# Splitting the context part from the expert part, and halving the first chain, in a one-core attention and expert kernel

## The chip, the core and the metric

The kernel runs on one core of one Trainium2 chip. The metric is the device time of one execution in microseconds. Every matrix and every intermediate is 32-bit float.

## The reference

```
B, T, D = 4, 512, 256                     # batches, tokens, width
# 1. conditioned bottleneck with residual, gain and offset per batch from cond (4, 128)
w_down = down_project * (cond @ down_gamma) + cond @ down_beta       # 256 x 64 per batch
w_up   = up_project * (cond @ up_gamma) + cond @ up_beta             # 64 x 256 per batch
h = relu(x @ w_down) @ w_up + x
# 2. attention over "paths": 8 heads, depth 5, causal
paths = sigmoid(h @ Wp + bp)                                         # 8 heads x 5
agree = pq * pk + (1 - pq) * (1 - pk)                                # per query, key, depth
sim = cumprod(agree, -1).sum(-1) / 5 ; attn = softmax(causal(sim))
ctx = attn @ (h @ Wv)                                                # heads joined, 256 wide
x = x + ctx @ Wo
# 3. low-rank decoder per batch, then the chosen expert
U = (cond @ W_dec + b_dec).reshape(B, 257, 30)
y = x @ (U[:, :256] @ V) + U[:, 256] @ V                             # rank 30
chosen = argmax(y @ gate_w.T)                                        # of 8 experts
x = x + y + y @ expert_w[chosen].T
```

## The kernel before

x is held transposed: 128 of the 256 features per partition block (two blocks, c), tokens along the free axis. The work is cut into **steps**, and one written list, `ORDER`, gives their order; every engine walks the same list and executes its own part of each step, so each engine runs its instructions in that order. There is no scheduler.

Steps of a batch b: `gdn` and `gup` compute the conditioned gains and offsets (TensorE) and form `w_dn` and `w_up` (VectorE); `down` is relu(x w_down), copied by ScalarE to `act_t`; `up` adds x and gives `h_t` (VectorE); `VL` (four, one per 128 tokens) gives values and path logits, copied by ScalarE to `v_sb`; `bias`, `tanh`, `feat` turn the logits into 32 sign products per head (VectorE, ScalarE, VectorE), a form in which the similarity is an inner product; `phi` transposes the features (TensorE) and scales them (ScalarE) to `phi_t`. Per batch six **pairs** (head group g of 4 heads, half of the queries) follow: `scores` (TensorE to the four banks of `s_ps`), the exponential to `prob` (ScalarE), the causal mask of diagonal tiles (GpSimd), and `context` (TensorE to `c_ps`), with row sums by a matmul with ones. VectorE takes the reciprocal and the product, which gives `ctx_t` (function `normalise`). In pairs 2 and 4 of a batch an `add` on VectorE sums two tiles before the row-sum matmul.

The expert part: `U` (four pieces) decodes U, SyncE moves it through DRAM into another layout, `Uadd` adds b_dec; `WoU` multiplies Wo by U; `zT` computes z = x U + ctx (Wo U), four products per token tile; `zs` transposes z and multiplies it with `Q` for the gate scores, VectorE picks the expert in six small instructions; `zo` (GpSimd, VectorE in the last batch) spreads z by the choice over 8 x 32 columns; `zoT` transposes that, ScalarE copies it to `zo_t`; `out` (four per batch: c and token half) accumulates ctx Wo and zo times `gexp` (from the `G` steps) in one bank, VectorE adds it into `x_t`, SyncE stores it.

Between the scores of one pair and of the next stand the **gaps**: `after_scores(b)` lists steps placed between scores p+1 and context p, `after_context(b)` steps between context p and scores p+2. They fill TensorE while ScalarE works on the exponential, since `s_ps` has one buffer. All steps of the gaps share two PSUM banks in turn (`WORK`): a step's matmuls wait until the step two before it has been emptied (`emptied`). The steps ahead of the first scores are in `PROLOGUE` and may also use the four banks of `s_ps` (`EARLY_BANK`). `WARM` matmuls on the identity run at the very start.

Loads before: SyncE's queue carries `first` (conditions, gamma, down_project), x of batch 0, `w_vl`, x of batches 1 to 3; ScalarE's queue carries `lift` at the start and, once relu of batch 0 is done, W_dec, `mix` and the experts; GpSimd issues the bias `bp_b` at 2.60 us and two small ones. A matmul of two 32-bit operands is two MATMUL records in the profile; nearly all of TensorE's instructions carry the helper's line L561 and are told apart by tile names.

Of the kernel before, what the change touches and what calls it, by code (L numbers as in the profile page):

```python
# [10 lines left out]
P = 128  # L11
# [3 lines left out]
HD = 64  # L15
# [15 lines left out]
WARM = 9  # L31
# [37 lines left out]
def adds(p):  # L69
# [10 lines left out]
EARLY_BANK = {("gdn", (0,)): 0, ("gup", 0): 1, ("down", 0): 2, ("gup", 1): 3, ("up", 0, 0): 4, ("up", 0, 1): 5,  # L80
              ("gdn", (1, 2, 3)): 0, ("VL", 0, 0): 1, ("VL", 0, 1): 2, ("VL", 0, 2): 3, ("VL", 0, 3): 4,
              ("gup", 2): 0, ("gup", 3): 1, ("phi", 0, 0): 5, ("phi", 0, 1): 2}


def after_scores(b):
# [17 lines left out]
    if prv >= 0:  # L103
        gaps[3] += [("zoT", prv, 0), ("zoT", prv, 1)]
# [3 lines left out]
def after_context(b):  # L108
# [28 lines left out]
for _b in range(B):  # L137
    for _i, (_a, _c) in enumerate(zip(after_scores(_b), after_context(_b))):
# [23 lines left out]
def build(nc, x_tr, first, lift, vl, mix, bp, W_dec, b_dec, expert_tr, out_tr):  # L162
    with ExitStack() as ctx:
# [43 lines left out]
        wo_u = sb("wo_u", [P, DC, B * KP])  # L207
# [147 lines left out]
        def _(act):  # L355
            act.dma_start(lift_sb[:], lift).then_inc(ld_lift, 16)
            for s in ORDER:
# [436 lines left out]
```

## Time and profile before

| what | value |
|---|---|
| three runs, median (lowest to highest) | 155.72 us (155.0 to 155.99) |
| profiled execution, its own time | 155.55 us |
| its span | 153.4 us |
| TensorE busy | 141.2 us, 92% |
| VectorE, ScalarE, GpSimd busy | 83.7, 58.8, 31.2 us |
| chain that ended last, by engine | TensorE 83%, VectorE 11%, ScalarE 2%, issue 1% |
| loads and stores | 12.50 MB, nearly all loads in the first 30 us |

The span is what the profile's instructions cover; the execution's time is 2.15 us more. "Busy" of TensorE counts pipelined matmuls with modelled ends. All times in rows are from the start of the span.

### The profile page before, as it was taken

The numbers are of one execution on the slowest core, as the hardware profiler recorded it, in microseconds if no ns is written. First come the engines' busy times: TensorE is split into PE (matmuls) and PEld (weight loads), VectorE is DVE, ScalarE is ACT, GpSimd is POOL, SyncE is SP. The second block draws the span as 40 slices with busy tenths as digits, with TensorE's granted clock in tenths as the row PEclk, the third lists the DMA queues.
The fourth block names the chain that finished last, engine by engine and source line by source line (L and its number), as shares of the span: only waits on it lengthen the run. The fifth ranks groups of instructions, "written<-read, shape, count | busy, mean of one in ns | idle before, by whom it ended". The sixth has DMA issues, their size and how long they took to land.

```text
span 153.4 us, 5078 instructions
## 1 busy us (share of the span) xinstructions
PE 141.2 (92%) x2296; PEld 89.8 (59%) x2296; DVE 83.7 (55%) x156; ACT 58.8 (38%) x70; POOL 31.2 (20%) x56
## 2 busy tenths in 40 slices
PE   5989678999497999999999999999999999999992
PEld 5746155554274777457656655567558577666650
DVE  0563532619966378296915483558146851985431
ACT  3013156264226342558333451573434447310010
POOL 7200004100405302640022205200222440110000
PEclk9999999999999999999999999999999999999999
DMA  4989999600011200000101000100011010110112
GB/s 121 311 320 433 448 376 353 209 4 0 0 22 17 35 0 4 0 4 0 37 3 38 34 4 0 38 0 4 34 38 38 0 38 0 38 38 34 68 38 71
DMA packets 7381, 12.50 MB, mean 81 GB/s; under 512 B 1552, under 2 KB 5808, under 8 KB 7232
## 3 DMA queue, kind: packets, MB, share of 16 engines
q10 hardware_dynamic: 2496, 7.23, 12.1%
q1 hardware_dynamic: 4768, 4.89, 9.9%
q0 software_dynamic: 96, 0.05, 1.1%
q8 instruction: 18, 0.29, 0.8%
q14 instruction: 3, 0.02, 0.1%
HBM read 9.95 MB, written 2.22 MB: 79 GB/s over the span
## 4 chain that ended last, share of the span: by engine, by line
PE 83%; DVE 11%; ACT 2%; issue 1%; POOL 0%; ACTq 0%; POOLq 0%; DVEq 0%
PE work L561 36%; PE c_ps L561 24%; PE s_ps L561 17%; PE work L738 3%; DVE rden L420 2%; DVE feat L552 2%; PE work L678 2%; DVE tiles L509 1%; ACT prob L365 1%; DVE h_t L455 1%; ACT phi_t L390 1%; DVE u_row L481 1%; PE work L730 1%; DVE x_t L541 1%; DVE logit L464 0%
## 5 line engine op out<-in xcount | busy, mean ns | idle before, releaser
L365 ACT ACTIVATE prob<-s_ps 128x1536 f32<-128x1536 f32 (+1 forms) x24 | 38.2, 1593 | 39.3 <-PE s_ps L561 36.3
L420 DVE RECIPROCAL rden<-c_ps 128x256 f32<-128x256 f32 x16 | 28.1, 1757 | 26.5 <-PE c_ps L561 26.5
L342 POOL TENSOR_SCALAR_AFFINE_SELECT prob<-prob 128x1024 f32<-128x1024 f32 x16 | 20.1, 1257 | 93.1 <-ACT prob L365 93.1
L561 PE MATMUL s_ps<-phi_t 32*128 32x256 f32 (+1 forms) x384 | 24.2, 365 | 1.6 <-ACT phi_t L390 1.0
L561 PE MATMUL c_ps<-prob,v_sb 128*32 128x256 f32 (+1 forms) x384 | 24.9, 346 | 0.0
L561 PEld LDWEIGHTS s_ps<-phi_t 32*128 32x128 f32 x384 | 17.4, 184 | 10.6 <-issue 6.8
L561 PE MATMUL work<-ctx_t,mix_sb 128*32 128x256 f32 x256 | 17.0, 381 | 0.4
L561 PE MATMUL work<-zo_t,gexp 128*32 128x256 f32 x256 | 16.9, 379 | 0.0
L561 PEld LDWEIGHTS c_ps<-prob,v_sb 128*32 128x32 f32 x384 | 11.5, 109 | 9.0 <-issue 2.0
L561 PE MATMUL c_ps<-prob,ones 128*32 128x256 f32 (+1 forms) x256 | 16.3, 326 | 0.0
L561 PE MATMUL work<-w_vl,h_t 128*32 128x296 f32 x208 | 14.8, 416 | 1.1 <-DVE h_t L455 0.6
L541 DVE TENSOR_TENSOR x_t<-work,x_t 128x256 f32<-128x256 f32 x16 | 6.7, 419 | 13.3 <-PE work L561 13.3
L561 PEld LDWEIGHTS work<-zo_t,gexp 128*32 128x32 f32 x256 | 8.6, 110 | 5.2 <-ACT zo_t L402 0.2
L561 PEld LDWEIGHTS work<-ctx_t,mix_sb 128*32 128x32 f32 x256 | 7.8, 110 | 4.9 <-ACT phi_t L390 1.2
L509 DVE TENSOR_TENSOR tiles<-prob 128x1024 f32<-128x1024 f32 x8 | 10.6, 1329 | 0.0
L561 PEld LDWEIGHTS work<-w_vl,h_t 128*32 128x32 f32 x208 | 6.1, 109 | 7.1 <-DVE pick L526 1.6
L561 PEld LDWEIGHTS c_ps<-prob,ones 128*32 128x32 f32 x256 | 8.0, 110 | 2.7
L350 POOL TENSOR_TENSOR zo<-z_nat,pick 128x256 f32<-128x256 f32 x12 | 7.0, 615 | 9.8 <-DVE pick L526 9.8
L377 ACT COPY v_sb<-work 128x296 f32<-128x296 f32 x13 | 5.2, 403 | 9.6 <-PE work L561 9.6
L455 DVE TENSOR_TENSOR h_t<-work,x_t 128x512 f32<-128x512 f32 x6 | 3.9, 686 | 8.2 <-PE work L561 8.2
L402 ACT COPY zo_t<-work 128x512 f32<-128x512 f32 x8 | 4.4, 590 | 8.4 <-PE work L738 8.4
L421 DVE TENSOR_TENSOR ctx_t<-c_ps,rden 128x256 f32<-128x256 f32 x16 | 6.8, 424 | 0.6
(95 smaller groups left out, 133.4 us busy)
## 6 DMA issues: line engine op xcount, KB each, us to landing
wdec<-in_W_dec ACTq DMA_DIRECT2D x1, 3855.0 KB, 15.2
x_t<-in_x_tr SPq DMA_DIRECT2D x4, 512.0 KB, 9.3
ex_t<-in_expert_tr ACTq DMA_DIRECT2D x1, 2048.0 KB, 22.1
out_x<-x_t SPq DMA_DIRECT2D x16, 128.0 KB, 1.7
mix_sb<-in_mix ACTq DMA_DIRECT2D x1, 776.0 KB, 16.8
lift_sb<-in_lift ACTq DMA_DIRECT2D x1, 384.0 KB, 3.7
w_vl<-in_vl SPq DMA_DIRECT2D x1, 296.0 KB, 4.9
first_sb<-in_first SPq DMA_DIRECT2D x1, 144.0 KB, 3.5
```

What stands on the lines that cost most here:

```text
L342: nc.gpsimd.affine_select(out=tri, in_=tri, compare_op=ALU.is_ge, fill=0.0, base=0, pattern=[[0, HG], [0, 2], [1, P]], channel_multiplier= ...
L350: ins = nc.gpsimd.tensor_tensor(zo[:, t], z_nat[:, t:t + 1, :].broadcast_to([P, E, KP]), pick[:, t, :].unsqueeze(2).broadcast_to([P, E, KP ...
L365: nc.scalar.activation(prob[:, p % 2, :, 0:width(p)], s_ps[:, :, 0:width(p)], ACT.Exp).then_inc(exped, 1)
L377: nc.scalar.copy(v_sb[:, b % 2, t, :], bank(s)[:, 0:D + H * DEPTH]).then_inc(empty(s), 1)
L402: nc.scalar.copy(zo_t[:, :, CW * s[2]:CW * (s[2] + 1)], bank(s)[:].rearrange("p (e t) -> p e t", e=2)).then_inc(empty(s), 1)
L420: link(nc.vector.reciprocal(rden[:], c_ps[m % 2][:, CW:2 * CW]))
L421: nc.vector.tensor_tensor(ctx_t[:, b % 2, g, CW * half:CW * (half + 1)], c_ps[m % 2][:, 0:CW], rden[:], ALU.mult).then_inc(ctx_ready, 1)
L455: nc.vector.tensor_tensor(h_t[:, :, half], bank(s)[:].rearrange("p (c t) -> p c t", c=DC), x_t[:, b, :, half], ALU.add).then_inc(empty(s), 1)
L509: nc.vector.tensor_tensor(tiles[:, chunk(p) % 2], both[:, :, 0, :], both[:, :, 1, :], ALU.add).then_inc(added, 1)
L541: nc.vector.tensor_tensor(x_t[:, b, c, half], bank(s)[:, 0:CW], x_t[:, b, c, half], ALU.add).then_inc(empty(s), 1)
L561: return nc.tensor.matmul(o, w, r, start=start, stop=stop, skip_group_check=True)
L738: ins = nc.tensor.transpose(o[:, CW * e + P * i:CW * e + P * (i + 1)], zo[:, 2 * hf + i, 4 * e:4 * e + 4, :].rearrange("p e k -> p (e k)") ...
```

## The change

- **First chain halved.** `bias`, `tanh`, `feat` and `phi` of batch 0 run once for token tiles 0 and 1 (`FIRST`) and once for 2 and 3 (`SECOND`); the first half's stand ahead of the first scores, the second half's `phi` behind scores 1. In every batch the `phi` copy of head group 1 is on VectorE instead of ScalarE. `gdn` of batches 1 to 3 comes before `up` of batch 0, its six VectorE instructions become two; `gup` 1 comes after `up`, `gup` 2 and 3 move into the gaps of batch 0. `WARM` is 8.
- **Early loads.** x of batch 0 comes in two halves, one on each queue (ScalarE's ahead of `lift`). W_dec comes in two halves of 64 partitions, one on each queue, issued at the start, as are `mix` (SyncE), the experts, x of batches 1 and 3 (ScalarE) and 2 (SyncE).
- **Context part as its own step.** New steps `mix` (four per batch, 16 records each) compute ctx Wo; VectorE adds them into `x_t` in place. `zT` reads only x (two products per token tile) and waits until the `mix` steps of its tokens are emptied. `out` keeps only the expert part (16 records) and is added into `x_t` again. `WoU`, its tile and the transposed Wo in `mix_sb` go.
- The gaps are filled anew, and the two banks start with the other one.

```diff
-WARM = 9
+WARM = 8
-PROLOGUE = [("gdn", (0,)), ("gup", 0), ("down", 0), ("gup", 1), ("up", 0, 0), ("up", 0, 1), ("gdn", (1, 2, 3)),
-            ("VL", 0, 0), ("VL", 0, 1), ("VL", 0, 2), ("VL", 0, 3), ("bias", 0), ("tanh", 0), ("feat", 0),
-            ("gup", 2), ("gup", 3), ("phi", 0, 0), ("phi", 0, 1), ("scores", 0), ("down", 1)]
+def features(b, ts):
+    return [("bias", b, ts), ("tanh", b, ts), ("feat", b, ts)]
+PROLOGUE = [("gdn", (0,)), ("gup", 0), ("down", 0), ("gdn", (1, 2, 3)), ("up", 0, 0), ("up", 0, 1), ("gup", 1),
+            ("VL", 0, 0), ("VL", 0, 1), *features(0, FIRST), ("VL", 0, 2), ("VL", 0, 3), ("bias", 0, SECOND),
+            ("phi", 0, 0, FIRST), ("phi", 0, 1, FIRST), ("tanh", 0, SECOND), ("scores", 0), ("feat", 0, SECOND),
+            ("down", 1)]
 def after_scores(b):
...
-        gaps[4] += [("phi", n1, 0), ("phi", n1, 1)]
+        gaps[4] += [("phi", n1, 0, ALL_T), ("phi", n1, 1, ALL_T)]
     if b == 0:
-        gaps[1] += [("VL", n1, 2), ("VL", n1, 3)]
-        gaps[2] += [("U", 1)]
-        gaps[3] += [("U", 3)]
-        gaps[5] += [("G", 1), ("Uadd",)]
+        gaps[0] = [("phi", b, 0, SECOND), ("phi", b, 1, SECOND)] + gaps[0]
+        gaps[1] += [("U", 0)]
+        gaps[2] += [("VL", n1, 2), ("VL", n1, 3)] + features(n1, ALL_T)
+        gaps[3] += [("U", 2)]
+        gaps[5] += [("gup", 3), ("Uadd",)]
...
     if prv >= 0:
+        gaps[0] += [("mix", prv, 2), ("mix", prv, 3)]
         gaps[3] += [("zoT", prv, 0), ("zoT", prv, 1)]
 def after_context(b):
...
     if b == 0:
-        gaps[0] += [("VL", n1, 0), ("VL", n1, 1)]
-        gaps[1] += [("bias", n1), ("tanh", n1), ("U", 0), ("feat", n1)]
-        gaps[2] += [("U", 2)]
-        gaps[3] += [("Q",)]
-        gaps[4] += [("G", 0), ("ubT",)]
-        gaps[5] += [("down", n2), ("WoU",)]
+        gaps[0] += [("gup", n2)]
+        gaps[1] += [("VL", n1, 0), ("VL", n1, 1)]
+        gaps[2] += [("U", 1)]
+        gaps[3] += [("Q",), ("U", 3)]
+        gaps[4] += [("G", 0), ("ubT",), ("mix", b, 0)]
+        gaps[5] += [("G", 1), ("down", n2), ("mix", b, 1)]
     else:
         gaps[0] += [("zT", prv, ALL_T)]
-        gaps[3] += [("out", prv, 0)]
-        gaps[4] += [("out", prv, 1)]
-        gaps[5] += [("out", prv, 2)]
+        gaps[2] += [("mix", b, 0), ("mix", b, 1)]
     if b >= 1 and n1 < B:
-        gaps[2] += [("bias", n1), ("tanh", n1), ("feat", n1)]
-    if prv >= 1:
-        gaps[1] += [("out", prv - 1, 3)]
+        gaps[2] += features(n1, ALL_T)
+        gaps[3] += [("out", prv, 0), ("out", prv, 1)]
+        gaps[4] += [("out", prv, 2)]
+        gaps[5] += [("out", prv, 3)]
...
     if b == B - 1:
-        gaps[2] += [("zT", b, FIRST)]
-        gaps[5] = [("zoT", b, 0), ("out", prv, 2), ("out", prv, 3)]
+        gaps[3] += [("zT", b, FIRST), ("out", prv, 0)]
+        gaps[4] += [("out", prv, 1)]
+        gaps[5] += [("zoT", b, 0), ("out", prv, 2), ("out", prv, 3)]
-ORDER += [("zT", B - 1, SECOND), ("out", B - 1, 0), ("zs", B - 1, SECOND), ("zo", B - 1, 1),
-          ("out", B - 1, 1), ("zoT", B - 1, 1), ("out", B - 1, 2), ("out", B - 1, 3)]
+ORDER += [("out", B - 1, 0), ("mix", B - 1, 2), ("mix", B - 1, 3), ("out", B - 1, 1), ("zT", B - 1, SECOND),
+          ("zs", B - 1, SECOND), ("zo", B - 1, 1), ("zoT", B - 1, 1), ("out", B - 1, 2), ("out", B - 1, 3)]
-        _k, _late = _late % 2, _late + 1
+        _k, _late = 1 - _late % 2, _late + 1
 # loads, SyncE
-            sp.dma_start(x_t[:, 0], x_tr[0].rearrange("(c p) t -> p c t", p=P)).then_inc(ld_x[0], 16)
+            sp.dma_start(x_t[:, 0, 0], x_tr[0, 0:P]).then_inc(ld_x[0], 16)
             sp.dma_start(w_vl[:], vl.rearrange("p (c n) -> p c n", c=DC)).then_inc(ld_vl, 16)
...
+            sp.dma_start(wdec[0:P // 2], W_dec[0:P // 2]).then_inc(ld_wdec, 16)
+            sp.dma_start(mix_sb[:], mix).then_inc(ld_mix, 16)
 # loads, ScalarE
+            act.dma_start(x_t[:, 0, 1], x_tr[0, P:2 * P]).then_inc(ld_x[0], 16)
             act.dma_start(lift_sb[:], lift).then_inc(ld_lift, 16)
...
+            act.dma_start(wdec[P // 2:P], W_dec[P // 2:P]).then_inc(ld_wdec, 16)
 # VectorE
+                elif kind == "phi" and s[2] == 1:
...
+                    nc.vector.tensor_scalar(phi_t[:, b % 2, g, tok], bank(s)[:, tok], rootc[:], None, op0=ALU.mult
+                                            ).then_inc(empty(s), 1)
-                elif kind == "out":
+                elif kind in ("mix", "out"):
 # TensorE
                 elif kind == "zT":
...
-                    pe.wait_ge(ctx_ready, BC * b + (NG if ts == FIRST else BC))
-                    for c in range(2 * DC):
+                    for i in range(TT):
+                        if i // DC in (t // 2 for t in ts):
+                            done(pe, ("mix", b, i))
+                    for c in range(DC):
                         for t in ts:
...
-                elif kind == "out":
+                elif kind in ("mix", "out"):
...
+                    for c in range(DC):
+                        w = wo[:, c, row] if kind == "mix" else gexp[:, c, row]
+                        r = ctx_t[:, b % 2, c, half] if kind == "mix" else zo_t[:, c, half]
+                        ins = tiled(o[:, 0:CW], w, r, start=(c == 0), stop=(c == DC - 1))
```

## Rows read from the trace of the kernel before

**Rows 1.** The page's first part: busy time and share of each engine.

```profile
PE 141.2 (92%) x2296; PEld 89.8 (59%) x2296; DVE 83.7 (55%) x156; ACT 58.8 (38%) x70; POOL 31.2 (20%) x56
```

**Rows 2.** Timeline, start to the third step (start us, us, engine, line, operation, output<-inputs, count).

```profile
1.59 4.21 PE L561 MATMUL c_ps<-ident 128*128 128x128 f32 x18 [1.59 <-POOL ident L316]
...
6.02 1.05 PE L561 MATMUL work<-lift_sb,cond_b 128*128 128x512 f32 x2
...
7.00 1.07 PE L561 MATMUL s_ps<-x_t,w_dn 128*32 128x256 f32 x16
...
9.06 1.14 PE L561 MATMUL s_ps<-act_t,w_up 64*128 64x256 f32 x8
...
10.13 0.94 PE L561 MATMUL work<-first_sb,cond_b 128*128 128x128 f32 x6
...
10.22 1.29 DVE L455 TENSOR_TENSOR h_t<-s_ps,x_t 128x512 f32<-128x512 f32 x2
...
11.66 1.21 PE L561 MATMUL work<-w_vl,h_t 128*32 128x296 f32 x16 [0.59 <-DVE h_t L455]
```

**Rows 3.** DMA issues (KB each, us to landing), then the stretch table's DMA share and GB/s.

```profile
lift_sb<-in_lift ACTq DMA_DIRECT2D x1, 384.0 KB, 3.7
...
bp_b<-in_bp POOLq DMA_DIRECT2D x1, 20.0 KB, 7.5
...
4.00:6.00 2.00, 2.00 (x11) 2.00 (x11) 0.91 (x3) 0.00 (x0) 0.86 (x2) 1.00 1.03 399
```

**Rows 4.** Timeline, bias of batch 0 to its first exponential.

```profile
16.42 0.33 DVE L464 TENSOR_TENSOR logit<-v_sb,bp_b 128x160 f32<-128x160 f32 x1 [3.60 <-ACT v_sb L377]
...
21.31 0.94 PE L561 MATMUL s_ps<-phi_t 32*128 32x256 f32 x16 [0.98 <-ACT phi_t L390]
...
22.31 1.45 ACT L365 ACTIVATE prob<-s_ps 128x1536 f32<-128x1536 f32 x1 [1.05 <-PE s_ps L561]
```

**Rows 5.** Groups of instructions by form: count | busy us, mean ns | idle before.

```profile
L552 DVE TENSOR_TENSOR feat<-feat,sign 128x512 f32<-128x512 f32 x4 | 2.8, 691 | 0.1
```

**Rows 6.** Waits of TensorE (engine line <- waited for: us in total, times, longest us).

```profile
PE work L561 <- DVE u_row L481: 2.2, 1, 2.2
```

**Rows 7.** Timeline, the z step of batch 1.

```profile
88.00 0.62 PE L561 MATMUL work<-x_t,u_w 128*32 128x128 f32 x16
...
88.43 0.62 PE L561 MATMUL work<-ctx_t,wo_u 128*32 128x128 f32 x16
```

**Rows 8.** Timeline, end of a context step and the output step behind it.

```profile
72.62 1.05 PE L561 MATMUL work<-ctx_t,mix_sb 128*32 128x256 f32 x16
...
72.88 1.76 DVE L420 RECIPROCAL rden<-c_ps 128x256 f32<-128x256 f32 x1 [0.97 <-PE c_ps L561]
...
74.47 0.94 PE L561 MATMUL s_ps<-phi_t 32*128 32x256 f32 x16
...
75.01 0.41 DVE L541 TENSOR_TENSOR x_t<-work,x_t 128x256 f32<-128x256 f32 x1
```

**Rows 9.** Timeline, last masked tile.

```profile
133.79 1.10 POOL L342 TENSOR_SCALAR_AFFINE_SELECT prob<-prob 128x1024 f32<-128x1024 f32 x1 [7.31 <-ACT prob L365]
...
135.13 0.61 PE L561 MATMUL c_ps<-tiles,ones 128*32 128x256 f32 x8
```

**Rows 10.** Timeline, expert chain of the last two token tiles, to the end.

```profile
142.15 0.36 ACT L398 ACTIVATE z_t<-work,ub_col 64x128 f32<-64x128 f32 x1 [3.89 <-PE work L561]
...
143.75 0.27 PE L730 MATMUL work<-ident,z_t 64*128 64x64 f32 x1
...
144.25 0.23 DVE L519 COPY z_nat<-work 128x64 f32<-128x64 f32 x1
...
145.42 0.76 DVE L534 TENSOR_TENSOR zo<-z_nat,pick 128x256 f32<-128x256 f32 x2
...
147.77 1.05 PE L561 MATMUL work<-zo_t,gexp 128*32 128x256 f32 x16
...
150.61 0.42 DVE L541 TENSOR_TENSOR x_t<-work,x_t 128x256 f32<-128x256 f32 x1 [1.30 <-PE work L561]
```

More of the change, by code:

```diff
@@ L76, with part @@
 ALL_T, FIRST, SECOND = (0, 1, 2, 3), (0, 1), (2, 3)
[L77 to L82 removed]
+def part(b, ts):
+    return 1 if ts == FIRST else b + 2
+def features(b, ts):
[4 more added lines that the diff above has]
+            ("down", 1)]
+EARLY_BANK = {("gdn", (0,)): 0, ("gup", 0): 1, ("down", 0): 2, ("gdn", (1, 2, 3)): 3, ("up", 0, 0): 4, ("up", 0, 1): 5,
+              ("gup", 1): 0, ("VL", 0, 0): 1, ("VL", 0, 1): 2, ("VL", 0, 2): 4, ("VL", 0, 3): 5,
+              ("phi", 0, 0, FIRST): 1, ("phi", 0, 1, FIRST): 2}
 def after_scores(b):
@@ L369, in _ @@
                     nc.scalar.activation(act_t[:], bank(s)[:, 0:T // 2], ACT.Relu).then_inc(empty(s), 1)
-                    if s[1] == 0:
-                        act.dma_start(wdec[:], W_dec).then_inc(ld_wdec, 16)
-                        act.dma_start(mix_sb[:], mix).then_inc(ld_mix, 16)
-                        act.dma_start(ex_t[:], expert_tr.rearrange("e (c p) f -> p e c f", p=P)).then_inc(ld_ex, 16)
                 elif s[0] == "VL":
@@ L491, in _ @@
                     ins.then_inc(u_ready, 1)
-                elif kind == "WoU":
-                    full(dve, s)
-                    nc.vector.tensor_copy(wo_u[:].rearrange("p c n -> p (c n)"), bank(s)[:, 0:DC * P]
-                                          ).then_inc(empty(s), 1)
                 elif kind == "G":
@@ L578, in scores @@
                 if p % BP < NG:
-                    done(pe, ("phi", b, g))
+                    done(pe, ("phi", b, g, ALL_T if b else FIRST))
+                elif b == 0 and first:
+                    done(pe, ("phi", b, g, SECOND))
                 for i, (kt, q0, n) in enumerate(units):
@@ L674, in _ @@
                 elif kind == "phi":
-                    _, b, g = s
-                    pe.wait_ge(feat_ready, b + 1)
-                    for t in range(TT):
+                    _, b, g, ts = s
+                    pe.wait_ge(feat_ready, part(b, ts))
+                    for t in ts:
                         ins = nc.tensor.transpose(
@@ L697, in _ @@
                     ins = nc.tensor.transpose(o[:, 0:B], ub_row[:].rearrange("b j k -> b (j k)"), ident[0:B, 0:B])
-                elif kind == "WoU":
-                    pe.wait_ge(u_ready, 1)
-                    pe.wait_ge(ld_mix, 16)
-                    for c in range(DC):
-                        for d in range(DC):
-                            ins = tiled(o[:, P * c:P * (c + 1)], wo_t[:, d, P * c:P * (c + 1)],
-                                        u_w[:, d].rearrange("p b k -> p (b k)"), start=(d == 0), stop=(d == DC - 1))
                 elif kind == "G":
@@ L740, in _ @@
                                 zo[:, 2 * hf + i, 4 * e:4 * e + 4, :].rearrange("p e k -> p (e k)"), ident[:])
-                elif kind == "out":
+                elif kind in ("mix", "out"):
                     _, b, i = s
-                    if b == 0 and i == 0:
-                        done(pe, ("G", 0))
-                        done(pe, ("G", 1))
                     row, half = slice(P * (i % DC), P * (i % DC + 1)), slice(CW * (i // DC), CW * (i // DC + 1))
-                    for c in range(2 * DC):
-                        if c == DC:
-                            done(pe, ("zoT", b, i // DC))
-                        w = wo[:, c, row] if c < DC else gexp[:, c - DC, row]
-                        r = ctx_t[:, b % 2, c, half] if c < DC else zo_t[:, c - DC, half]
-                        ins = tiled(o[:, 0:CW], w, r, start=(c == 0), stop=(c == 2 * DC - 1))
+                    if kind == "mix":
+                        if b == 0 and i == 0:
+                            pe.wait_ge(ld_mix, 16)
+                        pe.wait_ge(ctx_ready, BC * b + NG * (i // DC + 1))
+                    else:
+                        if b == 0 and i == 0:
+                            done(pe, ("G", 0))
+                            done(pe, ("G", 1))
+                        done(pe, ("zoT", b, i // DC))
+                    for c in range(DC):
+                        w = wo[:, c, row] if kind == "mix" else gexp[:, c, row]
+                        r = ctx_t[:, b % 2, c, half] if kind == "mix" else zo_t[:, c, half]
+                        ins = tiled(o[:, 0:CW], w, r, start=(c == 0), stop=(c == DC - 1))
                 ins.then_inc(filled, 1)
@@ L777 @@
         "vl": halves(np.concatenate([a["attn_Wv"], a["attn_Wp"]], axis=1)),
-        "mix": np.concatenate([halves(a["attn_Wo"]), halves(a["attn_Wo"].T), v4, halves(v4.T),
+        "mix": np.concatenate([halves(a["attn_Wo"]), v4, halves(v4.T),
                                halves(a["ffn_gate_w"].T)], axis=1),
```

90 lines of the change are left out of this document (47 added, 43 removed).

## The prediction

> **What bounds the kernel now.** I read the page's first part first: TensorE is busy for 92% of the span, the next engine (VectorE) for 55% [rows 1]. So outside a few places the time is TensorE's work plus the gaps in it, and a change is worth what it takes from either. Then the timeline of the start: TensorE waits in turn for VectorE and ScalarE from its first useful matmul to the first scores at 21.31 [rows 2, 4]. That stretch is a chain, not work. The table of waits shows the one large gap after it: 2.2 us behind a VectorE copy of U in batch 0 [rows 6]. Last the end of the timeline: the expert part of the last two token tiles is a chain over four engines, but full output steps stand between its links, and TensorE hardly stops before 150.61 [rows 10].
>
> **The start.** One warm-up matmul less takes 2 of 18 records off 4.21 us, 0.4 to 0.47 us [rows 2]. What follows it is gup of batch 0, which needs lift. Lift now stands on ACT's queue behind one half of x of batch 0 (256 KB). First, both halves of x and lift are 144+512+384 KB, 1.06 million bytes. Before, lift was in SBUF 3.7 us after its issue at 0.81, and the queues move 399 GB/s then [rows 3]; 262 KB put ahead of it cost 0.65 us at that rate, and a larger share for x's other half on SP about as much again. I take 5.95 for lift where it was 4.5, so gup's matmul starts at 6.1 to 6.2 against 6.02, and down at 7.1 against 7.00 [rows 2]. Bounds: 0.4 us gained if lift lands by 5.4, 0.3 lost if it comes at 6.3. I take 0.1 lost.
> The Trainium skill ("DMA: Bandwidth & Descriptors", section "Queues, rings and completion order") says that a DMA engine goes round the queues in whole packets of several descriptors, not one descriptor at a time. By that first and the first half of x would not be served evenly and lift could land earlier or later than my even split; both fall inside the bounds above.
>
> gdn of batches 1 to 3 takes the place of gup 1 before up. Its 6 records take 0.94 [rows 2]; its two VectorE operations, now over three batches at once, are an estimate of 0.56 each between the 0.42 of a 256-element add and the 0.69 of a 512-element one [rows 5, 8]. They end at about 10.15, just where up's result is there anyway (1.16 us after up's start, 9.06 to 10.22) [rows 2]. So h_t starts within 0.1 us of before, and VL at 11.6.
>
> The halved chain is the gain. VL steps follow at 1.0 us each from 11.66 [rows 2], and the first half needs two of them, not four. Bias of the first half is at 14.4 instead of 16.42 [rows 4]. Its features lose the largest step of 0.69 [rows 5] and the others shrink, about 0.55 in all; phi is copied 256 wide, one group on ScalarE and the other on VectorE beside it, at about the 0.4 of a 256-element add [rows 8]. Scores 0 starts at about 17.85, **3.45 us ahead** of 21.31. U's weights are now asked for at the start; U(0) is not before 27, and the 9.5 MB of loads are in by about 26 at 399 GB/s, so the early weights themselves are worth nothing: nobody waited for them before either.
>
> **Batch 0, where the lead goes.** TensorE works on two banks in turn, so each step waits for the step before last to be emptied, in the order of the engine that empties it.
> (a) gup 2 and gup 3 stood in TensorE's idle time of the start; now they stand in full stretches, 2 x 1.0 [rows 2]. The second halves of phi 0 add 0.5 behind the first scores. Two mix steps of batch 0 come into it, 2 x 0.87: an old output step of 32 records runs from 72.62 to 74.47, 1.74 plus 0.11 for the change of tile shape, and a mix or a new out step is half of it [rows 8]. WoU goes, twice the 0.43 that 16 such records take [rows 7]: -0.87. Together +3.4.
> (b) Gone: the wait for the U copy, -2.2 [rows 6].
> (c) up(1,0) takes the bank of phi's second half, which ScalarE empties only after exponential 1. That runs 1.0 us after scores 1 starts and takes 1.45 [rows 4]; TensorE is through with phi 1.4 us after that start, and up may go 2.85 after it: +1.45.
> (d) mix(0,0) waits for G(0)'s VectorE add: +0.5. mix(0,1) has the bank of G(1), whose add stands on VectorE behind the normalisation of the context step ahead. Such a normalisation and the add after it end 2.8 us after TensorE is free of the context: reciprocal from 72.88 for 1.76, the product to about 75.1, then the add at 75.01 to 75.42, while TensorE was free at 72.6 [rows 8]. Between them TensorE has only G(1) and down(2), 1.74: with the U sum ahead, +1.2.
> (e) Five more changes of tile shape at 0.1: +0.5.
> Sum +4.85, so scores 7 comes 1.4 us later than before.
>
> **Batches 1 to 3, up to the last scores.** Halves of output steps done by then: 21 where 18 were (without the two above), +2.6. Four z steps lose 0.43 each [rows 7], -1.7. New gaps: mix(b,2) takes the bank of up(b+2,0), emptied by h_t's first half at 1.16+0.69+0.05 = 1.9 us after up's start, while TensorE is free after 1.07 [rows 2, 5]: 2 x 0.83. phi after two out steps that both wait for the normalisation: 2 x 0.15. Batch 3 has no up and no VL to fill: mix(2,2) comes 0.6 before its normalisation, scores after context 19 come 0.25 before exponential 20 is done, mix(3,0) waits 0.1. Together +2.9. Scores 23 is at +5.2.
>
> **The end.** The mask of the last pair ends at 134.89 in the old times and the context matmuls started at 135.13, right behind a full output step [rows 9]; with half a step ahead TensorE waits 0.7 and starts 0.1 earlier at most. Then zoT, three half outs, two mixes and one half out, 0.58 + 6 x 0.87, and 0.45 for a bank: the last z step starts at 143.15 in old times. From there nothing stands beside the chain: z's matmuls and z_t 1.0, the transposed product 0.55 (143.75 to 144.25, and its hand-over), scores to zo 1.17, zo to the matmul on zo_t 2.35, two half outs and their drain 0.87+1.05, [rows 10], 7.05 in all: 150.2, -0.4 against 150.61. It has 4.35 us less work than before, and the bare chain eats that: some 4.1 us of it TensorE idles.
>
> **Sum.** 153.4 + 5.2 - 0.4 = 158.2, and 2.15 lie around the span in the profiled execution (155.55), which is 0.17 under the median of 155.72. That gives **160.3 us**, 3% more.
>
> **Rivals.**
> (1) Faster: VectorE's order does not hold the banks. Every gap of (c), (d), the two up steps and batch 3 rests on a copy or add that stands behind an exponential, a reciprocal or h_t. They are 1.45+0.5+1.2+1.66+0.3+0.95, 6.1 us; if all go, 154.2, and with the end's bank 153.8, over 1% faster. For it: VectorE is idle for 45% of the span [rows 1]. Against it: the positions come from the order written out, and the old output add did wait for the normalisation [rows 8]. It decides only from nearly the whole 6.1. Chance 0.1.
> (2) The gaps are there but half as large, since each delay pushes the next wait into cover: 160.3-3.1 = 157.2, at the edge of 1%. Chance 0.25.
> (3) Slower still: 16 more VectorE adds of 0.42 [rows 8] meet the masks on GpSimd (1.10 each, 16 of them [rows 9]), and each meeting lengthens one of the two; if half of them cost 0.4 us on the path, 163. Chance 0.08. The Trainium skill ("SBUF — State Buffer", section "Who interferes with whom") lets only a VectorE operation with two SBUF inputs, or one in a two-port mode, lock GpSimd out, and these adds read PSUM and SBUF; by it this rival costs nothing, which is why its chance is small.
> (4) The warm-up is too short: the 18 records run 0.22 apart, while gdn's six of the same 128-column form run 0.13 apart [rows 2], so TensorE came up from the lower level (1.2 of 2.4 GHz, where the granted clock reads full) only after them. If it comes up a step later, gup and down take twice 1.0 and 0.87: +1.9, 162.2. Chance 0.07.
> (5) The early weights hold up the small bias load, which shares the DMA engines. It landed 7.5 us after its issue at 2.60 [rows 3], 10.1, and is wanted at 14.4, so 4 us are to spare; beyond that each us is one. Chance 0.03, at 161.5.
>
> **How the numbers follow.** The forecast itself (158.4 to 161.8) has 0.47. A measurement of this kernel tells about 1% from no change, 154.2 to 157.3. Rival 1 puts 0.08 below it; rival 2 about 0.12 inside and the rest above. Since a sum of so many small waits can miss a cover, I move a little from slower to the others: faster 0.11, same 0.16, slower 0.73. The range goes from 156.0, inside rival 2, to 162.5, which takes in rivals 4 and 5.
>
> **What would show it.** Scores 0 at 17.9; down 0 at 7.1; a TensorE wait of 1.4 us for phi_t before up in batch 0; one of about 1.2 for gexp; 0.8 for h_t in two batches; PE busy near 138; some 4 us idle between the last z step and the last two outs. Wrong would be: scores 7 before 55.18, or a last z step that starts less than 6.5 us before the last add.

## The result, and the profile after

The changed kernel takes **188.53 us**, the median of four runs (187.43 to 190.3); the kernel before, run beside it, takes 155.53 (155.0 to 155.99). The ratio is 1.21, with a 95% interval of 1.2028 to 1.2171. The forecast was 160.3 with a range up to 162.5: the sign was right, the size was not, and most of what made the size is not in the prediction's sum at all.

The page's parts 1, 2 and 4 of the kernel after [rows 1]:

```profile
PE 142.4 (77%) x2198; PEld 87.1 (47%) x2198; DVE 91.5 (49%) x178; ACT 56.8 (31%) x68; POOL 31.5 (17%) x56
...
PE   6900000795799988978899999889999898989834
...
ACT  0000000235434433312543454155345334631010
...
PEclk9995555599999999999999999999999999999995
...
PE 54%; DVE 18%; ACTq 17%; DMA 3%; ACT 3%; issue 3%; SPq 1%; DVEq 0%
```

TensorE is busy for about as long as it was (142.4 us against 141.2; a little of it at a lower clock, below), but over 185.3 us of span in place of 153.4. ScalarE does nothing for seven slices, and in the chain of work that ended last its sequencer (ACTq, the part of ScalarE that issues instructions and DMAs) stands for 17%. The timeline of the start shows where:

```profile
3.65 28.29 ACTq L373 DMA_DIRECT2D x_t<-in_x_tr  x1
...
6.11 1.29 PE L579 MATMUL work<-lift_sb,cond_b 128*128 128x512 f32 x2 [0.31 <-DMA lift_sb<-in_lift]
...
7.33 1.07 PE L579 MATMUL s_ps<-x_t,w_dn 128*32 128x256 f32 x16
...
31.97 1.28 ACT L386 ACT_TABLE_LOAD   x1 [31.97 <-issue]
33.27 0.38 ACT L386 ACTIVATE act_t<-s_ps 128x256 f32<-128x256 f32 x1
...
33.80 2.09 PE L579 MATMUL s_ps<-act_t,w_up 64*128 64x256 f32 x8 [24.53 <-ACT act_t L386]
```

gup and down come nearly as in rows 2 (6.11 and 7.33). Then relu of batch 0, an ordinary instruction of ScalarE, does not run, for ScalarE's sequencer is still in the **issue** of its sixth and last load, x of batch 3: that one instruction takes 28.29 us. The five issues ahead of it take 0.42 to 0.82 us. Such a row is not the transfer itself (for the same load it is 0.50 us long in an experiment below): the engine stands in front of its queue, and relu runs only once the row is over. The table of DMA issues [rows 3] says what the queues were doing:

```profile
ex_t<-in_expert_tr ACTq DMA_DIRECT2D x1, 2048.0 KB, 35.6
...
wdec<-in_W_dec SPq DMA_DIRECT2D x1, 1927.5 KB, 17.3
wdec<-in_W_dec ACTq DMA_DIRECT2D x1, 1927.5 KB, 28.8
...
mix_sb<-in_mix SPq DMA_DIRECT2D x1, 520.0 KB, 28.5
...
lift_sb<-in_lift ACTq DMA_DIRECT2D x1, 384.0 KB, 4.8
...
bp_b<-in_bp POOLq DMA_DIRECT2D x1, 20.0 KB, 10.3
```

ACT's W_dec half, asked for at 2.24, landed at 31.0; the blocked issue ended at 31.94. The stretch table shows that these loads moved at half the rate of rows 3, and what the pause did to TensorE's granted clock:

```profile
12.00:16.00 4.00, 0.00 (x0) 0.00 (x0) 0.00 (x0) 0.00 (x0) 0.00 (x0) 0.66 0.95 187
16.00:20.00 4.00, 0.00 (x0) 0.00 (x0) 0.00 (x0) 0.00 (x0) 0.00 (x0) 0.50 0.99 219
...
32.00:36.00 4.00, 2.20 (x9) 1.49 (x10) 0.12 (x1) 1.64 (x2) 0.00 (x0) 0.50 1.09 350
```

The DMA engines are busy for 99% of the time at 219 GB/s, where rows 3 has 399. And up runs at the lower level of TensorE's clock (granted 0.50): 2.09 us for the 8 records that took 1.14 in rows 2.

From the first scores on the kernel does much what was forecast. First its waits of TensorE [rows 6]; then the first scores [rows 4], and a mix step that waits for gexp, with the scores behind it [rows 8]:

```profile
PE s_ps L579 <- ACT act_t L386: 24.5, 1, 24.5
PE work L751 <- DVE zo L550: 2.1, 1, 2.1
PE work L579 <- DVE gexp L514: 1.7, 2, 1.3
...
PE work L579 <- DVE h_t L468: 1.5, 2, 0.8
PE work L579 <- ACT phi_t L405: 1.4, 1, 1.4
```

```profile
43.70 0.94 PE L579 MATMUL s_ps<-phi_t 32*128 32x256 f32 x16 [0.58 <-DVE phi_t L485]
...
80.75 0.41 DVE L514 TENSOR_TENSOR gexp<-work,mix_sb 128x256 f32<-128x256 f32 x1
81.22 1.07 PE L579 MATMUL work<-ctx_t,mix_sb 128*32 128x256 f32 x16 [1.32 <-DVE gexp L514]
82.22 0.94 PE L579 MATMUL s_ps<-phi_t 32*128 32x256 f32 x16
```

The span is 31.9 us longer, and it adds up so: scores 0 start at 43.70 for 21.31, +22.4 (24.5 of waiting and about 1 for the slower up, less the forecast lead of some 3.4); scores 0 to 23 take 119.2 for 110.0, +9.2, where the forecast has +8.7; the rest +0.3.

The end [rows 10]:

```profile
175.34 0.36 ACT L413 ACTIVATE z_t<-work,ub_col 64x128 f32<-64x128 f32 x1 [5.59 <-PE work L579]
...
177.48 0.76 DVE L550 TENSOR_TENSOR zo<-z_nat,pick 128x256 f32<-128x256 f32 x2
...
179.78 2.94 PE L579 MATMUL work<-zo_t,gexp 128*32 128x256 f32 x32 [0.77 <-ACT zo_t L417]
...
182.77 0.42 DVE L557 TENSOR_TENSOR x_t<-work,x_t 128x256 f32<-128x256 f32 x1 [1.28 <-PE work L579]
```

### The profile page after: what moved, and what is told of

It reads as the page before. It is cut to its first block, busy times and chain, and to the rows that moved or that the text cites. A ratio compares the mean times of both kernels' runs of the same rounds, so it can differ in the third digit from the quotient of the medians.

```text
span 185.3 us, 4942 instructions
## 1 busy us (share of the span) xinstructions
PE 142.4 (77%) x2198; PEld 87.1 (47%) x2198; DVE 91.5 (49%) x178; ACT 56.8 (31%) x68; POOL 31.5 (17%) x56
## 4 chain that ended last, share of the span: by engine, by line
PE 54%; DVE 18%; ACTq 17%; DMA 3%; ACT 3%; issue 3%; SPq 1%; DVEq 0%
PE work L579 24%; PE c_ps L579 16%; ACTq L373 15%; DVE rden L435 9%; PE s_ps L579 9%; DMA u_scratch<-u_row 2%; PE work L751 2%; DVE ctx_t L436 2%; PE work L698 1%; DMA u_raw<-u_scratch 1%; ACT prob L382 1%; DVE x_t L557 1%; DVE h_t L468 1%; ACT L386 1%; DVE feat L569 1%
## 5 line engine op out<-in xcount | busy, mean ns | idle before, releaser
L354 POOL TENSOR_SCALAR_AFFINE_SELECT prob<-prob 128x1024 f32<-128x1024 f32 x16 | 20.8, 1298 | 117.3 <-ACT prob L382 117.3
L579 PEld LDWEIGHTS s_ps<-phi_t 32*128 32x128 f32 x384 | 17.3, 184 | 10.8 <-issue 8.0
L557 DVE TENSOR_TENSOR x_t<-work,x_t 128x256 f32<-128x256 f32 x32 | 13.2, 422 | 18.4 <-PE work L579 18.4
L579 PE MATMUL s_ps<-act_t,w_up 64*128 64x256 f32 x8 | 2.1, 667 | 24.5 <-ACT act_t L386 24.5
L579 PE MATMUL work<-ctx_t,mix_sb 128*32 128x256 f32 x256 | 15.6, 381 | 4.3 <-DVE gexp L514 1.7
L579 PE MATMUL work<-zo_t,gexp 128*32 128x256 f32 x256 | 17.3, 399 | 1.0 <-ACT zo_t L417 0.8
L579 PEld LDWEIGHTS c_ps<-prob,v_sb 128*32 128x32 f32 x384 | 12.0, 110 | 8.6 <-issue 1.4
L468 DVE TENSOR_TENSOR h_t<-s_ps,x_t 128x512 f32<-128x512 f32 x2 | 1.3, 686 | 25.4 <-PE s_ps L579 25.4
L579 PEld LDWEIGHTS s_ps<-act_t,w_up 64*128 64x128 f32 x8 | 1.3, 321 | 24.8 <-issue 24.7
L525 DVE TENSOR_TENSOR tiles<-prob 128x1024 f32<-128x1024 f32 x8 | 9.9, 1237 | 0.0
## 6 DMA issues: line engine op xcount, KB each, us to landing
wdec<-in_W_dec SPq DMA_DIRECT2D x1, 1927.5 KB, 17.3
wdec<-in_W_dec ACTq DMA_DIRECT2D x1, 1927.5 KB, 28.8
x_t<-in_x_tr SPq DMA_DIRECT2D x1, 512.0 KB, 29.8
```

What stands on the lines that cost most here:

```text
L354: nc.gpsimd.affine_select(out=tri, in_=tri, compare_op=ALU.is_ge, fill=0.0, base=0, pattern=[[0, HG], [0, 2], [1, P]], channel_multiplier= ...
L468: nc.vector.tensor_tensor(h_t[:, :, half], bank(s)[:].rearrange("p (c t) -> p c t", c=DC), x_t[:, b, :, half], ALU.add).then_inc(empty(s), 1)
L525: nc.vector.tensor_tensor(tiles[:, chunk(p) % 2], both[:, :, 0, :], both[:, :, 1, :], ALU.add).then_inc(added, 1)
L557: nc.vector.tensor_tensor(x_t[:, b, c, half], bank(s)[:, 0:CW], x_t[:, b, c, half], ALU.add).then_inc(empty(s), 1)
L579: return nc.tensor.matmul(o, w, r, start=start, stop=stop, skip_group_check=True)
```

## The experiments

Two questions: what holds ScalarE's sequencer, and what the change is worth without that. All ratios are to the kernel before, run beside each.

**One load off ScalarE's queue.** Of the changed kernel:

```diff
-            act.dma_start(x_t[:, 3], ...)        # ACT's sixth load
+            sp.dma_start(x_t[:, 3], ...)         # last on SP
```

> The changed kernel with one load moved: x of batch 3 is issued last on SyncE instead of last on ScalarE. Theory A (the whole surprise is that ScalarE's sequencer stood in this one issue, 28.3 us in the trace): ScalarE is free from 3.7 us, relu of batch 0 comes at about 8.5, and the time falls to the forecast's 160.3 plus what late loads cost (x of batch 1 landed at 20.8 where down(1) now wants it at 18.7, +1.6; W_dec landed at 31.0 where U(0) wants it at 29, +1.8) plus 1.0 for the lower clock of the last two output steps: about 164.5. Rival B (the loads themselves are too slow and ScalarE would have waited for something else): stays above 180. Rival C (SyncE blocks in the same way): nothing computes on SyncE, so it would show as a long issue there and no loss.

Measured, four runs: 166.37 us (165.19 to 169.07), ratio 1.0621 (1.0538 to 1.0703). No issue on ScalarE takes over 0.82, scores 0 start at 17.67. So 22.2 us of the 33 were that one issue. A new wait stands in the trace, for x of batch 1, which lands late:

```profile
PE work L579 <- DMA x_t<-in_x_tr: 3.7, 1, 3.7
```

**Before, with the new loads only.** This takes the order of the steps out of it:

```diff
-            sp.dma_start(...)                    # before's loads of SP and ACT
+            ...                                  # after's loads, same order and queues
```

> The kernel before with only the loads of the changed one (both queues, same order, same splits; its wider mix block is kept) and its own step order. Theory A: relu of batch 0 comes at about 33 instead of 8.1 and the kernel takes 155.5 + 25 + about 1.5 for the clock that has fallen by then, 182. If the block needs something of the new step order, it stays near 156 to 160.

Measured, one run: 185.65 us, 3.7 over the 182 expected. The queue rows and TensorE's first wait:

```profile
2.81 0.83 ACTq L361 DMA_DIRECT2D ex_t<-in_expert_tr  x1
...
3.66 30.80 ACTq L362 DMA_DIRECT2D x_t<-in_x_tr  x1
```

```profile
PE s_ps L563 <- ACT act_t L375: 27.0, 1, 27.0
```

The new loads alone make the old kernel 29.8 us slower, without any of the new step order.

**What the issue waits for.** The experts go as 2048 rows of 1 KB. One run lays them out as 128 rows of 16 KB, another only swaps them with x of batch 3:

```diff
-            act.dma_start(ex_t[:], expert_tr.rearrange("e (c p) f -> p e c f", p=P))
+            act.dma_start(ex_t[:], expert_tr)    # host layout: p e c f
```

> The changed kernel with the experts laid out on the host so that their load is 128 rows of 16 KB and not 2048 rows of 1 KB. Same bytes, same number of loads, same order. If the issue of x of batch 3 blocks because too many rows are queued ahead of it, it takes about 0.5 us here and the kernel runs in about 164.5. If it blocks because a sixth load is outstanding, or because of the bytes, the issue again takes over 25 us and the time stays near 188.

```diff
-            act.dma_start(ex_t[:], ...)
             act.dma_start(x_t[:, 3], ...)
+            act.dma_start(ex_t[:], ...)
```

> The changed kernel with the last two loads on ScalarE swapped: x of batch 3 fifth, the experts sixth. Rows in total are the same. If the limit is on the rows queued when the next load is issued (experts' 2048 ahead of it), nothing blocks now: the experts are last, 832 rows are ahead of them, and the time is about 164.5. If whole loads must fit (2880 rows in all) or the sixth load is the one that blocks, the experts' issue takes over 15 us and the time stays above 175.

Measured: 168.0 and 165.12 us, one run each. ScalarE's last issues, in the run with 128 rows and then in the swapped one:

```profile
2.79 0.83 ACTq L372 DMA_DIRECT2D ex_t<-in_expert_tr  x1
...
3.65 0.50 ACTq L373 DMA_DIRECT2D x_t<-in_x_tr  x1
```

```profile
2.80 0.81 ACTq L372 DMA_DIRECT2D x_t<-in_x_tr  x1
...
3.64 0.54 ACTq L373 DMA_DIRECT2D ex_t<-in_expert_tr  x1
```

With the same bytes in the same six loads nothing blocks, once the rows are few or once nothing is issued behind the 2048 rows. So neither bytes nor the number of loads hold the sequencer; it is an issue behind many queued rows. How many rows a queue takes was not measured: the swapped run shows only that the same rows go through when the long list is the last.

**W_dec by columns.** The halves of 64 partitions were the suspect for the rate. On top of the first experiment:

```diff
-            sp.dma_start(wdec[0:P // 2], W_dec[0:P // 2]); act.dma_start(wdec[P // 2:P], W_dec[P // 2:P])
+            N = (D + 1) * K // 2
+            sp.dma_start(wdec[:, 0:N], W_dec[:, 0:N]);     act.dma_start(wdec[:, N:], W_dec[:, N:])
```

> As the run with x of batch 3 on SyncE, and W_dec's two halves are cut along its columns (all 128 partitions each, 15.4 KB per row) and not along its partitions. Theory A: the halves of 64 partitions load at half rate (2.2 us a row and 210 to 220 GB/s in the trace of the changed kernel, where the kernel before had 1.15 us a row and 400), and that is what makes x of batch 1 and W_dec late. Then x of batch 1 lands by about 13, W_dec by about 20, TensorE's wait of 3.7 us for x goes, and the kernel takes 161 to 162. Rival B (two queues share the engines badly whatever the split): x of batch 1 still lands near 20 and the time stays at 166.

Measured: 162.74 (162.62 to 164.26), ratio 1.0466 (1.0406 to 1.0525); the wait for x is gone. The same stretches of the table, with the halves by partitions (first experiment) and then by columns:

```profile
12.00:16.00 4.00, 3.71 (x60) 2.04 (x52) 1.40 (x7) 1.66 (x5) 0.00 (x0) 1.00 1.07 204
16.00:20.00 4.00, 1.57 (x20) 1.15 (x20) 2.27 (x8) 2.14 (x4) 0.00 (x0) 0.86 1.03 197
```

```profile
12.00:16.00 4.00, 3.65 (x60) 2.39 (x64) 1.47 (x6) 1.42 (x4) 0.00 (x0) 1.00 1.01 429
16.00:20.00 4.00, 2.67 (x44) 1.56 (x36) 3.00 (x11) 1.54 (x5) 0.00 (x0) 1.00 0.96 395
```

Equally busy engines, twice the bytes. The edit also halves the length of W_dec's rows, from 30 KB to 15 KB, but that is not it: the kernel before loads the same 30 KB rows over all 128 partitions, and its stretches from 8 to 20 us have 386 to 439 GB/s. The Trainium skill ("SBUF — State Buffer", section "Door 1: The DMA port swizzle") says that a DMA's rate depends on how many of the 16 ports of SBUF its partitions reach, and that the partition's bit for 64 picks one of two ports of a cluster: a half of 64 partitions reaches half of them. These rows agree, at 197 to 204 against 395 to 429 GB/s. Nor did the two halves make up for each other: in the changed kernel SyncE's half was in 17.3 us after its issue and ScalarE's 28.8. The prediction cited the page for another matter and did not ask it this.

This run is the changed kernel as the prediction imagined it. Its scores 7 and 23 start at 56.96 and 137.62, where the forecast gives 56.6 and 136.5.

**Before, with sound early loads.**

```diff
-            act.dma_start(wdec[:], W_dec) ...    # behind relu of batch 0
+            ...                                  # all loads at the start, as in the run by columns
```

> The kernel before, with only its loads changed to those of the column-split run (nothing blocks, full rate). If early weights are worth nothing by themselves, this is 155.5 to 156.2 (lift lands later and moves the first chain by about 0.3). If they are worth something, it is below 154.5.

Measured: 156.85 (155.83 to 157.97), ratio 1.0067 (1.0031 to 1.0102); scores 0 at 21.32, as before. Loading early gains nothing. The profiled run (157.86) had two stretches with a granted clock of 0.67 and 0.72. Most of the 0.7% goes with that clock: of the ten runs the four with a mean granted clock of 0.997 or more took 155.83 to 156.26, the six with 0.989 or less 156.56 to 157.97.

**The halved chain alone.** Before, with the first chain halved, the merged gdn, `WARM` 8 and gup 2 and 3 in the prologue; loads, z, out and the other gaps as before:

```diff
-            ("VL", 0, 2), ("VL", 0, 3), ("bias", 0), ("tanh", 0), ("feat", 0), ("phi", 0, 0), ...
+            ("bias", 0, FIRST), ("tanh", 0, FIRST), ("VL", 0, 2), ("feat", 0, FIRST), ...
+        gaps[0] += [("phi", b, 0, SECOND), ("phi", b, 1, SECOND)]
```

> The kernel before, its loads, its z, its output steps and its gaps, with only the halved first chain (bias, tanh, features, phi of batch 0 in two halves, phi of head group 1 on VectorE, merged gain operations, 8 warm-up matmuls); gup 2 and 3 stay in the stretch ahead of the second scores and the second half of phi comes behind up. The step of the forecast: scores 0 about 3.5 us ahead (17.6 to 18.1), and since nothing else is added the lead carries through: 152.0 to 153.3. Rival: the lead is given back in batch 0 as in the changed kernel, 155 to 156.

Measured, four runs: 155.58 (153.35 to 156.24), ratio 0.989 (0.9818 to 0.9963). The profile is of a run of 156.08, and in it the lead is gone by batch 0's end. Against the kernel before, scores 0 are 2.9 us ahead (18.44), scores 1 2.5, scores 2 to 4 only 0.9 (the second halves of phi stand between, with 0.7 of waits for h_t), and scores 5 are 0.8 late (45.68 for 44.87). That last step is the clock. Both kernels have the same wait of 2.2 us for U's copy, and behind it the granted clock was 1.00 in the trace of before and 0.66 here, in these two rows of the stretch table:

```profile
40.00:45.00 5.00, 3.39 (x58) 2.17 (x62) 3.47 (x6) 1.88 (x1) 0.00 (x0) 1.00 0.07 11
```

```profile
40.00:45.00 5.00, 4.26 (x50) 2.38 (x50) 2.08 (x5) 1.88 (x1) 0.00 (x0) 0.66 0.05 8
```

Before with early loads, at 0.67 from 20 to 25 and 0.72 here, has scores 5 at 47.29, 2.4 late. So this one trace doesn't say what the halved chain is worth: the only run of the four with a mean granted clock of 1.00 took 153.35, close to the 152.0 to 153.3 expected, and it has no trace.

**The end reordered.** On the kernel by columns, one step at a time stands between the links of the last expert chain:

```diff
-        gaps[5] += [("zoT", b, 0), ("out", prv, 2), ("out", prv, 3)]
+        gaps[5] += [("zoT", b, 0), ("out", prv, 2)]
-ORDER += [("out", 3, 0), ("mix", 3, 2), ("mix", 3, 3), ("out", 3, 1), zT, zs, zo, zoT, ("out", 3, 2), ("out", 3, 3)]
+ORDER += [("mix", 3, 2), ("mix", 3, 3), ("out", 2, 3), zT, ("out", 3, 0), zs, zo, ("out", 3, 1), zoT,
+          ("out", 3, 2), ("out", 3, 3)]
```

> The column-split run with only the end reordered: the last two mix steps and the last z step first, then the outs of token half 0 behind z's parts, so that VectorE's choice of the expert runs beside two half outs. The forecast's step: 4.1 us of bare chain at the end, of which 2.5 to 3 can be covered, and the clock that has fallen for the last two outs (1.0) with it. Expected 3 to 4 us below the column-split run. If the end does not bind, no change.

Measured: 160.08 (159.62 to 160.62), ratio 1.0268 (1.0235 to 1.0301), 2.7 us less than by columns. The last two outs, by columns and then here:

```profile
154.53 3.55 PE L579 MATMUL work<-zo_t,gexp 128*32 128x256 f32 x32 [0.77 <-ACT zo_t L417]
```

```profile
153.30 1.93 PE L580 MATMUL work<-zo_t,gexp 128*32 128x256 f32 x32 [0.77 <-ACT zo_t L418]
```

By columns the granted clock is 0.75 over the last 5.7 us, here it stays at 1.00. Of the 2.7 us, 1.6 are this and 1.2 the shorter wait for zo (0.9 for 2.1); against them stands a new wait of 0.8 for ctx_t ahead of the last mix steps. Another 0.8 is not the edit's: scores 0 start at 17.70 for 18.50, since the first gup took 1.92 us by columns and 1.12 here, with the same instructions.

**Batch 0's order.**

```diff
-        gaps[0] = [("phi", b, 0, SECOND), ("phi", b, 1, SECOND)] + gaps[0]
+        gaps[0] += [("phi", b, 0, SECOND), ("phi", b, 1, SECOND)]         # behind up
-        gaps[5] += [("G", 1), ("down", n2), ("mix", b, 1)]
+        gaps[5] += [("down", n2), ("G", 1), ("mix", b, 1)]
```

> The column-split run with two swaps in batch 0: phi's second halves behind up and not ahead of it, and down(2) ahead of G(1) so that mix(0,1) no longer takes G(1)'s bank. The forecast's steps (c) and (d): TensorE's 1.4 us wait for phi_t and 1.2 us for gexp go; phi then waits up to 0.7 for h_t. Expected 1.5 to 2.6 below the column-split run (160.1 to 161.2). If those waits come back elsewhere, no change.

Measured: 159.75 (158.85 to 160.25), ratio 1.026 (1.0217 to 1.0303). Scores 7 at 54.35 for 56.96, of which 0.9 is an earlier scores 0 (17.57) and 1.7 the new order. The wait for phi_t ahead of up is gone, and that for gexp is 0.4 where two made 1.7; a new one of 0.9 for h_t ahead of phi stands against them:

```profile
PE work L698 <- DVE h_t L468: 0.9, 2, 0.8
...
PE work L579 <- DVE gexp L514: 0.4, 1, 0.4
```

Both waits were worth what the prediction gave them, and about a third of it comes back elsewhere.

**All repairs together,** with mix(b,2) and mix(b,3) ahead of up as well:

```diff
-        gaps[0] += [("mix", prv, 2), ("mix", prv, 3)]
+        gaps[0] = [("mix", prv, 2), ("mix", prv, 3)] + gaps[0]
```

> The column-split run with the batch-0 swaps, the reordered end, and mix(b,2), mix(b,3) ahead of up, so that neither waits for h_t's bank (0.83 in each of two batches). If the forecast's account of the changed order is right, all of this adds up: 162.7 - 2.7 (end) - 2.0 (batch 0) - 1.3 (up) = 156.7, about the kernel before and not below it: what the change takes from TensorE's work is then given back by the shorter covers that remain.

Measured: 158.13 (157.96 to 158.22), ratio 1.0161 (1.0126 to 1.0197), 1.4 over the 156.7 expected. The move of mix was worth nothing: from scores 7 to scores 13 it is 31.7 us with it and 31.8 without. The waits for h_t ahead of mix are gone, but up, now behind the mix steps, waits for their banks inside: in batch 1 its 8 records take 1.75 us for 1.29. With loads, waits and end mended, the version that adds the context apart is still 1.6% slower than before. Its sum of U also waits for the DRAM trip of the next experiment (0.7 us on VectorE); moving that sum was not tried here.

**The halved chain with the changed order of U,** on top of the halved chain alone:

```diff
-        gaps[1] += [("VL", n1, 2), ("VL", n1, 3)]       # after scores 1, batch 0
+        gaps[1] += [("U", 0)]
-        gaps[2] += [("U", 1)]
-        gaps[3] += [("U", 3)]
+        gaps[2] += [("U", 1), *features(n1, ALL_T)]
-        gaps[1] += [bias, tanh, ("U", 0), feat]         # after context 1, batch 0
+        gaps[1] += [("VL", n1, 2), ("VL", n1, 3)]
-        gaps[3] += [("Q",)]
+        gaps[3] += [("Q",), ("U", 3)]
```

> The halved chain alone, with batch 0's gaps filled as the changed kernel fills them (U(0) behind scores 2, batch 1's VL behind context 1, its features beside context 2, U(3) behind context 3), which took the 2.2 us wait for the U copy away. Old z, old output steps, old loads. Expected: that wait gone in the trace, 1.5 to 2 below the halved chain alone, 152 to 153.5, and so below both kernels. Rival: the wait is replaced by one for Q's or phi's bank and nothing is gained.

Measured, twelve runs: 156.3 (155.17 to 156.82), ratio 1.0025 (0.9997 to 1.0053); the 2.2 us wait is gone, the gain did not come. Scores 6 are at 46.41, 3.4 ahead of before, scores 7 at 55.19, level with it. The timeline in between, with ScalarE's and TensorE's rows left out but one:

```profile
43.92 2.32 SPq L310 DMA_DIRECT2D u_scratch<-u_row  x4
49.03 0.94 SPq L314 DMA_DIRECT2D u_raw<-u_scratch  x2
53.28 0.48 DVE L507 TENSOR_TENSOR u_w<-u_raw,bdec 128x120 f32<-128x120 f32 x2 [4.42 <-DMA u_raw<-u_scratch]
53.68 1.75 DVE L433 RECIPROCAL rden<-c_ps 128x256 f32<-128x256 f32 x1
...
53.87 1.39 PE L581 MATMUL work<-u_w,mix_sb 128*32 128x128 f32 x32 [2.89 <-issue]
```

U's way through DRAM takes 9.4 us from its first issue (in the other traces 7.8 to 9.0), and it begins no sooner than before (43.64 there), although the scores are 3.4 us ahead. VectorE stood 4.4 us in the sum that waits for it, with the reciprocal behind, and TensorE 2.9 in WoU. "issue" in that last row is not what it waits for; the row of VectorE above names it.

**That sum and WoU later.**

```diff
-        gaps[5] += [("G", 1), ("Uadd",)]         # after scores 5, batch 0
+        gaps[5] += [("G", 1)]
-        gaps[5] += [("down", n2), ("WoU",)]      # after context 5, batch 0
+        gaps[5] += [("down", n2), ("Uadd",)]
+    if prv == 0: gaps[0] += [("WoU",)]           # batch 1, behind up
```

> The kernel before with the halved first chain and the changed batch 0 order as in the run with chain and U order, but the sum of U with its decoder row on VectorE moved from behind scores 6 to behind the last halves of down, and the WoU step from there to batch 1's first gap behind up. Theory (U's trip through DRAM, stored at 43.92 and back at 53.28, stood in front of VectorE's normalise and of WoU and ate the lead of 3.4 us that stood at scores 6): TensorE's 2.9 us of idle time ahead of WoU goes, scores 7 start by about 51.8 where they started at 55.19, and the time is 152.5 to 153.5. Rival (something else takes the lead as soon as this wait is gone, a wait for h_t's bank or the lower granted clock of the stretch 55 to 60): scores 7 at 54 or later and a time of 155 to 156.5.

Measured, six runs: **152.39** (152.0 to 153.05), ratio 0.9793 (0.9757 to 0.9829): the fastest version, about 2% faster than before. Scores 7 at 50.46, sooner than the 51.8 expected; granted clock 1.00 over the whole span. The same places:

```profile
49.73 1.76 DVE L435 RECIPROCAL rden<-c_ps 128x256 f32<-128x256 f32 x1 [1.31 <-PE c_ps L583]
...
52.46 0.48 DVE L509 TENSOR_TENSOR u_w<-u_raw,bdec 128x120 f32<-128x120 f32 x2 [0.51 <-DMA u_raw<-u_scratch]
...
53.60 1.08 PE L583 MATMUL work<-u_w,mix_sb 128*32 128x128 f32 x32 [1.13 <-DVE h_t L468]
```

The reciprocal no longer stands behind the DRAM trip, and VectorE waits 0.5 for it. TensorE's 2.9 is 1.1, a wait for h_t's bank. From scores 8 to 23 this kernel takes 71.7 us, exactly as before; scores 23 at 128.50 for 131.27 is a lead of 2.8, about what the halved chain gave, now kept. Of the 3.9 us to the run before it, 0.45 are an earlier scores 0 and about 1 is the granted clock, 1.00 for 0.71 in the stretch from 55 to 60; most of the rest goes with the wait.

## Why the prediction failed, point by point

**The step that failed** is the sentence "U's weights are now asked for at the start; U(0) is not before 27, and the 9.5 MB of loads are in by about 26 at 399 GB/s, so the early weights themselves are worth nothing". It asked only when the data would be there, and failed twice. First, the moved loads are instructions of ScalarE ahead of relu, and one of them could block: no row of before has a load issued behind the 2048 rows of the experts, so its cost had no bound in the trace, and I put none on it. It costs 22.2 us. Of ScalarE's issues the prediction priced bytes ahead of lift, not the issues themselves. Second, 399 GB/s was read off loads over 128 partitions and used for halves of 64: 197 to 219 GB/s, the experts in at 38.4 and not 26. It costs 3.6 us once the first is mended.

**Lift, gup, down:** lift landed at 6.1 (4.8 after its issue at 1.27; forecast 5.95, though its terms add up to 5.8), inside the bounds, down started at 7.33 (7.1). The first gup took 1.05 us before; in the eleven traces with `WARM` 8 it took 1.12 to 1.92, 1.77 in the halved chain alone, although the granted clock reads 1.00 there. That is rival 4 in part: the shorter warm-up gains 0.34 us at down in the last experiment (6.66 for 7.00) and loses 0.9 by columns (7.89).

**The first chain:** scores 0 at 17.57 to 18.64 where nothing blocks, the two latest behind a first gup of 1.9 us (forecast 17.85). Right.

**Batch 0 and later:** with 25.4 us taken off (the wait of 24.5 and the slower up), scores 7 of the changed kernel is at 56.8 (forecast 56.6) and scores 23 at 137.5 (136.5), one more. Term (b), the 2.2 us wait, went as said. The waits named were there: phi_t 1.4 (1.45), gexp 1.3 and 0.4 (1.2 and 0.5), h_t twice 0.8 (0.83), and zo 2.1. Rival 1 (order does not hold the banks) and rival 2 (the gaps are half as large) are refuted by these rows; and the experiment with batch 0's order bought 1.7 of 2.7 us back. Its mate, mix ahead of up, did not: that wait moved into up. PE busy was to be near 138: it is 142.1 by columns, and 139.8 with the end reordered, where the granted clock stays at 1.00.

**Rival 3** (adds meeting the masks): the masks took 1298 ns on average over 16, but already 1257 before (rows 9 shows one of the short ones, 1.10), and 1210 in the last experiment, which has the old number of adds. So the new adds cost GpSimd 0.7 us in all at most, and no wait of TensorE names the masks.

**The end:** from the last z step, 8.1 us against 7.05. The chain of links was right: TensorE is idle for 3.4 us between its links (some 4 forecast). But behind that it ran the last 32 records in 2.94 us for 1.93, at a granted clock of 0.56 over the last 5 us. The idle time was priced, what follows it was not.

**The sum** for the kernel imagined is 2.4 us short: 160.3 forecast, 162.74 measured by columns, 0.2 over the range's end. Scores 23 a microsecond late and the clock at the end (3.55 us for 1.93) account for it. For the kernel given, the sum missed one step worth about five times its whole effect of 4.8 us. (It adds 2.15 to the span and names, but does not add, the 0.17 to the median.)

## What to carry to other kernels

A load moved to the start is first an instruction of the engine that issues it: count the rows already in that queue, put the load with the most rows last, and keep what the compute engine must do first ahead of it or the loads on an engine with nothing to do. A lead won at the start survives only if each fixed delay further on, like a trip through DRAM, is given as much more distance; look which engine stands first in line for it and what is queued behind. Splitting work at a price of equal TensorE time and more bank turns pays only where a wait goes with it, and in none of the runs here did the split of the context part earn its price. Compare the granted clock of two traces before you give a difference to an order of steps.

## What the runs showed of the hardware

- An issue behind a load of 2048 rows of 1 KB took 28.29 and 30.80 us; behind the same bytes as 128 rows 0.50. While it lasts the engine runs nothing.
- While a half of W_dec went into 64 partitions, the loads moved 187 to 219 GB/s; with both halves over 128 partitions 395 to 429, with the DMA engines equally busy.
- A pause of TensorE can cost twice. With none of its work in the rows from 12 on, the granted clock read 0.66 and then 0.50, and the next up took 2.09 us for 1.14. After 3.4 us of idle links at the end, 32 records took 2.94 and 3.55 for 1.93. After 2.9 us of waiting the stretch 55 to 60 had 0.71. It does not come each time: behind the same wait of 2.2 us the stretch 40 to 45 had 1.00 in the kernel before and 0.66 in the halved chain alone.
